# A transformer-like block on one core: the order of a turn's stages written out as two strings

## The reference, cut to what matters

```
x = x + attn_a(layernorm(x))   # 16 heads of 8 channels, softmax over all 1024 keys, output projection
x = x + ffn(layernorm(x))      # signs +-1 as weights: 128 -> 512 -> 512 -> 128, relu, scales s0, s1, s2
x = x + attn_b(layernorm(x))   # 8 heads of 16: for each token distances to the last 64 tokens under a learnt metric,
                               # the 32 nearest of them, weights exp(-distance), a weighted mean of values,
                               # a gate, times q, and a decoder matrix
x = x + ffn(layernorm(x))
```

## Time and profile before

| | |
|---|---|
| time, median of 3 runs | 2957.09 us (2952.42 to 2960.92) |
| profiled execution, span | 2956.4 us, 60895 instructions |
| PE busy | 2416.3 us (82%) |
| ACT busy | 2258.2 us (76%) |
| DVE busy | 2096.8 us (71%) |
| POOL busy | 732.5 us (25%) |
| phase one of TURN1 | 273.5 to 438.4 us |
| phases one of the six turns after it, sum | 1056.8 us |
| phases two of TURN1 to the last of `TURNS` (six), sum | 1025.5 us |
| phase two of TURN7 | 157.8 us |
| before TURN1, and the tail after TURN7 | 273.5 us and 277.9 us |

### The profile page before, as it was taken

The page is one execution under the profiler, slowest core; times in us unless marked ns, Lnnn a source line. Parts: engine busy times, 40 slices in busy tenths (PEclk is TensorE's granted clock), DMA queues, the critical chain, the costliest instruction groups (busy, mean ns, idle before and its releaser), DMA issues.

```text
span 2956.4 us, 60895 instructions
## 1 busy us (share of the span) xinstructions
PE 2416.3 (82%) x21171; PEld 1045.7 (35%) x21171; DVE 2096.8 (71%) x10258; ACT 2258.2 (76%) x3159; POOL 732.5 (25%) x933
## 2 busy tenths in 40 slices
PE   4788778888788887888888887888878888888666
PEld 1112233244332443334422443324433344324444
DVE  5801768957787668966799577876679666992585
ACT  4798668977699677987789776996769877895543
POOL 3020115211251114401162112511134111321442
PEclk6599789999899999999999998999989999999887
DMA  3011001100011001210011000110012000000000
GB/s 88 30 49 40 2 19 48 50 18 6 23 56 43 18 10 27 65 31 9 19 44 54 18 6 23 54 42 17 6 26 74 31 9 13 11 20 1 16 20 12
DMA packets 98519, 84.79 MB, mean 29 GB/s; under 512 B 19955, under 2 KB 79541, under 8 KB 98213
## 3 DMA queue, kind: packets, MB, share of 16 engines
q1 hardware_dynamic: 97968, 80.41, 9.3%
q10 hardware_dynamic: 244, 0.49, 0.1%
HBM read 55.32 MB, written 25.44 MB: 27 GB/s over the span
## 4 chain that ended last, share of the span: by engine, by line
PE 34%; ACT 34%; DVE 18%; issue 6%; POOL 6%; SPq 2%; DMA 1%; ACTq 0%; DVEq 0%; POOLq 0%
PE banks L849 31%; ACT PT L1188 17%; DVE xn L1535 4%; ACT pq L1175 3%; DVE h L1538 3%; DVE pq L1322 2%; ACT hparts L1199 2%; POOL Aop L820 2%; ACT h L1200 2%; ACT xn L1133 2%; PE banks L856 2%; ACT h L1101 1%; ACT Bs L1101 1%; POOL qkf L761 1%; DVE stat L1296 1%
## 5 line engine op out<-in xcount | busy, mean ns | idle before, releaser
L1188 ACT ACTIVATE PT<-banks 128x1024 f32<-128x1024 f32 x1024 | 996.6, 1038 | 51.0 <-PE banks L849 47.4
L1322 DVE CUSTOM_DVE_ANT_0 pq<-pq,banks 128x512 f32<-128x512 f32 x1024 | 653.5, 684 | 182.5 <-ACT pq L1175 182.0
L1175 ACT ACTIVATE pq<-banks 128x1024 f32<-128x1024 f32 x512 | 522.9, 1022 | 226.2 <-PE banks L849 201.0
L849 PE MATMUL banks<-PT,Vg 128*9 128x512 f32 x4096 | 545.0, 604 | 2.2 <-ACT PT L1188 2.2
L849 PE MATMUL banks<-Q,K 51*128 51x512 bf16 x2048 | 391.7, 393 | 139.7 <-ACT PT L1188 113.4
L849 PE MATMUL banks<-K,Q 48*128 48x512 bf16 x2048 | 361.6, 431 | 84.8 <-ACT pq L1175 38.0
L801 POOL TENSOR_TENSOR hparts<-h,hparts 128x512 fp32r<-128x512 f32 x108 | 135.6, 1272 | 995.2 <-ACT h L1200 995.2
L1535 DVE MATCH_REPLACE8 xn<-h,xn 128x96 f32<-128x96 f32 x1536 | 354.3, 256 | 0.0
L849 PE MATMUL banks<-hparts,W 128*128 128x512 f32 x992 | 291.4, 421 | 35.0 <-ACT h L1200 24.4
L849 PEld LDWEIGHTS banks<-Q,K 51*128 51x128 bf16 x2048 | 96.4, 93 | 619.1 <-ACT PT L1188 526.8
L1538 DVE MAX8 h<-xn 128x8 f32<-128x96 f32 x1536 | 264.3, 251 | 0.0
(11 more groups left out here) (217 smaller groups left out, 3330.6 us busy)
## 6 DMA issues: line engine op xcount, KB each, us to landing
Vw<-scratch_v SPq DMA_DIRECT2D x256, 51.0 KB, 2.1
scratch_k<-pq SPq DMA_DIRECT2D x24, 384.0 KB, 3.1
K<-scratch_k SPq DMA_DIRECT2D x126, 72.0 KB
qkf<-in_hidden_states SPq DMA_DIRECT2D x16, 512.0 KB, 4.4
scratch_q<-pq SPq DMA_DIRECT2D x24, 256.0 KB, 2.3
Q<-scratch_q SPq DMA_DIRECT2D x126, 48.0 KB
K<-scratch_k SPq DMA_DIRECT2D x126, 48.0 KB
scratch_v<-Bs SPq DMA_DIRECT2D x8, 544.0 KB, 3.6
```

The lines of the kernel that those rows point to most:

```text
L849: return pe.matmul(o, l, r, start=start, stop=stop)
L1175: act.activation(cut(g), ring_pair if work is TURN0 and g % 2 else pair[0], ACT.Relu).then_inc(diff_out.sem, 1)
L1188: act.activation(PT[:, at:at + 2, :], pair[g % ESLOTS], ACT.Exp, scale=1.0 if i % 8 < 4 else -1.0).then_inc(probs.sem, 1)
L1322: dve.tensor_tensor_reduce(r, r, pair[1 + g % 2][:, par, :], 1.0, -3.0e38, ALU.subtract, ALU.max, mred[:, par, i, qt:qt + 1]).then_inc(max ...
```

## The change

`phases` still merges the two parts as before. For the turns with sides behind (`behind`: TURN1, the five of `TURNS` and TURN7) each merged part is then re-ordered by a string. A letter names a line of work: `m` max and mrow, `t` mturn, `v` the value projections, `x` exp, `s` pvs and pvo (the eviction of a quad's result), `r` residual, `l` the four loads of `h`, and `o`, `p`, `q`, `h` the other stages of those sides. Within a line of work the order stays as it was; only how the lines are interleaved comes from the string. A letter with no line in this turn is skipped. Ring numbers are counted anew from the new list. No instruction is added or dropped.

```
+from collections import deque
...
+ORDER_ONE = (
+    "mqooqqoooqmooqomoqqmvqqqqmvooqqqqqqmooomoomqqqqqpomoooomoqqmqqmoqqqqmoqmqpmqmqqmqmqqmqqmpqqmqqqmpqqqqmqqqmppqqmq"
+    "qpmpqqmqmqqmpmpptmppppppmpppmmpppmppmppmpppmpmppmppppmpppqmptppmppppmppppmppmppmppmppmpmppmpppmptmppmpmppmppmppm"
+    "pppmppmppmppmppmppmpppmppmpppmm")
+ORDER_TWO = (
+    "hpxxpxxsxxhhsxxsxppxhhpppsxxpspxxphsxsppppxhxxpspxppxpssphxpxsptxxspxxpspppxxsxppppxhppsxxppphpxsxsxpxspsxxsxppp"
+    "xxsppxppsxpxpspppxsxppppxxpsxxsxxsspxppsxpxppxppsxpsppppxxppxppsxxsxpxsxxspsxpxsxxppppxssxxppppspppxppppxxspxxsx"
+    "xpppsxxsxxpssxpppxsxppppspphhxxpppxpsxxspxlxpspxxsppxxsxxppspsxxplpsxppxsppxxsxxppxsspxpxlxprpspxsxxpxsppspxxlpp"
+    "xssxpxxsxxsxxsxppxspsspp")
...
+def letter(work):
+
+    side, stage = work[:2]
+    if side == "a":
+        return dict(max="m", mrow="m", mturn="t", v="v", exp="x", pvs="s", pvo="s", residual="r")[stage]
+    return "l" if stage == "load" else side
+
+
+def woven(letters, order):
+
+    lines = {}
+    for work in order:
+        lines.setdefault(letter(work), deque()).append(work)
+    out = [lines[at].popleft() for at in letters if at in lines]
+    assert not any(lines.values()) and len(out) == len(order)
+    return out
...
     order = merged(*one) + merged(*two)
+    if behind:
+        order = woven(ORDER_ONE, merged(*one)) + woven(ORDER_TWO, merged(*two))
```

## The result

The changed kernel takes 2784.9 us (median of 4 runs, 2781.4 to 2791.3) against 2955.9 for the kernel before in the same runs: ratio 0.9434, 95% interval 0.9414 to 0.9455. The forecast was 2916, its range ended at 2872.

| us | before | after | change |
|---|---|---|---|
| six phases one with side `q` | 1056.8 | 974.7 | -82.1 |
| phase one of TURN1 | 164.9 | 152.3 | -12.6 |
| six full phases two | 1025.5 | 952.8 | -72.7 |
| phase two of TURN7 | 157.8 | 155.0 | -2.8 |
| ahead of TURN1, and the tail | 551.4 | 549.6 | -1.8 |

The account below looks back on a forecast made before the run. It took ACT to bound phase two and PE phase one. From 2957 us, phase two would give 48 and phase one cost 7, making 2916; the forecast's own range was 2895 to 2938, the full range 2872 to 2955.

Parts of the forecast that it names:

- 10.87 us of stalls: Phase two, first third: four ACT stalls, before `mT`, `xTa` and two exps, would all go, out of 16.5 us idle.
- The floor of 159 to 161: Full phase two: shortest length expected, ACT's 155.4 us of work plus 3.5 to 5.6 us of remaining idle time.
- Fifteen places: from 1 us (nearly all covered) to 7 us (none covered); I take 3.: Phase two: moved `pvs` stages would make ACT wait for PE, costing 3 us a phase, from 1 to 7.
- The lower bound of 30 us for phase two: Least total gain claimed for all phases two, whose forecast gain was 48 us with bounds 30 to 66.
- Cover: 4 us.: Phase boundary: the residual, biased by 164.3 us, would be ready 4 us before the next `wo` wants it at 168.
- Rival 4: Phase boundary: SP later than reckoned makes the residual late; 8 us late gives 2940 us; chance 0.03.
- which frees DVE of 2.15: Phase two, unit 4: moving POOL's bias add to the very end would spare DVE's stretched L1553 2.15 us.
- Taking the larger of the two engines and 1.79 in each interval gives 182.6 before and 183.9 after: Phase one, gaps between neighbouring `max` stages: a cost rule giving 1.3 us more a phase; 7 us booked in all.
- rival 3: Phase one: clumped side stages make PE wait at the ring, 9 us more in each of seven phases; 2972; chance 0.09.
- about 1 us each: Phase one: gain for each hand-over between side stages that stood back to back and now comes apart.
- The rival that phase one gains as well: Phase one: regrouped stages let PE work ahead of ACT, 5 us in each of seven phases; 2875; chance 0.17.
- The clock, counted as nothing in phase one: PE clock: about 1.3 us saved twice at phase two's `dist` was left uncounted; phase one's costing had no clock term.

Follow-up runs that it names:

- two_h: Kernel before with only side `h`, up to its third split, moved in phase two to the string's places; 2925.7 us, ratio 0.9920.
- two_pt: Kernel before with only side `p` and the last `mturn` moved in phase two to the string's places; 2918.3 us, ratio 0.9900.
- two_pth: Kernel before with side `p`, the last `mturn` and `h` up to its third split moved in phase two; 2877.1 us, ratio 0.9767.
- two_t: Kernel before with only the last `mturn` of phase two moved, from 3 to 22 exps ahead of it; 2949.6 us, ratio 0.9996.
- after_pvs: Changed kernel with `pvs` and `pvo` of phase two back at the old counts of exps; 2793.1 us, ratio 0.9476 to the kernel before.
- after_res: Changed kernel with the residual load moved up, ahead of the loads of quads; 2766.2 us, ratio 0.9382 to the kernel before.
- one_hand: Kernel before with seven `max` stages of phase one shifted to stand between seven back-to-back pairs of side stages; 2950.0 us, ratio 0.9997.
- one_only: Kernel before with the string for phase one alone, phase two keeping its merged order; 2849.2 us, ratio 0.9660.
- one_sides: Kernel before with phase one's side stages in the string's order, `max`, `mrow` and `mturn` keeping old counts of side stages ahead; 3016.2 us, ratio 1.0229.
- one_maxes: Kernel before with `max`, `mrow` and `mturn` of phase one at the string's counts of side stages ahead, side order old; 2894.8 us, ratio 0.9814.
- one_queue: Phase-one string alone, but three `max` stages moved from ahead of `lnn` to behind it; 2865.3 us, ratio 0.9725 to the kernel before.
- one_close: Phase-one string alone, but six `max` stages taken from between six pairs of side stages; 2872.1 us, ratio 0.9748 to the kernel before.
- one_hand2: Kernel before with ten phase-one `max` stages shifted: ahead of `lnn` and `lnT` at three layernorms, three more in quad 0; 2937.7 us, ratio 0.9959.
- one_sides2: Kernel before with phase one's side stages and `mturn` in the string's order, `max` and `mrow` keeping old counts; 2963.9 us, ratio 1.0058.

## Why the prediction was wrong

**Phase two, mechanism right.** 10.87 us of stalls were to leave; ACT's idle time fell by 10.4 a phase (15.5 to 5.1). The 33rd exp begins 45 to 46 us into a phase where it began 52 to 56 in: 6 to 11 of the 9 to 14 us that a phase is shorter lie ahead of it, and 2 to 3 more behind it. POOL's three hand-overs were the cause, as two_h, two_pt and two_pth show together; `mturn`, at which the largest stall stood, was not (two_t). The floor of 159 to 161 is where the phase ended: 158.8.

**The term that failed in phase two: "Fifteen places: from 1 us (nearly all covered) to 7 us (none covered); I take 3."** The sign was wrong. after_pvs shows +1.3 us a phase when the old places are put back. 163 less 3 less 1.3 is 158.7, the measured length, so this term is the whole miss in phase two (27 us in seven phases). I priced each place as if PE reached it at the same moment as ACT. Why none costs was not tried; one reading is that PE, freed of its stalls, is ahead of ACT there. The lower bound of 30 us for phase two was also added up wrongly: with 7 us paid back in each of seven phases its own terms leave 20 (and 62 with 1 us).

**The residual: "Cover: 4 us."** SP's queue was reckoned well: over the six phases the issue comes 152.9 to 156.3 us in (157 forecast), lands 5.8 to 7.4 us later (4.9 forecast), and the add ends at 161.6 to 165.6 (164.3 forecast). It was set against a phase two of 163 us, and the phase came out at 158.8: the 4 us that phase two gained beyond the forecast were the cover. Rival 4 gave a late residual a chance of 0.03, by a late SP; the shorter phase did it. The forecast also took the add's new place as free ("which frees DVE of 2.15"), and in four of six turns it cost about as much there. after_res prices both at 19 us.

**Phase one: the step "Taking the larger of the two engines and 1.79 in each interval gives 182.6 before and 183.9 after" failed.** It is responsible for 102 of the 131 us between 2916 and 2785 (+7 forecast, -94.7 measured). Its sum for before was already 6 us above the measured length of the list that it was to describe. (The 22 us of PE's waits in rival 3 and in the text on one_hand are low too: they sum to 26.0 in the phase at 956.9.) The same rule can be worked out for two more of the lists (estimates, with one cost for each kind of stage):

| list | rule, us a phase | measured |
|---|---|---|
| before | 182.6 | 176.1 |
| one_only | 183.9 | 158.8 |
| one_sides | 183.7 | 186.9 |
| one_maxes | 188.4 | 168.9 |

The first three lie within 1.3 us of each other where the measured ones span 28, and the one put last is the second fastest. The tight places it counted are no worse in the new order. PE's waits in a phase of before, and then of one_only (us in total, times, longest):

```profile
PE banks L849 <- ACT h L1200: 4.6, 5, 1.6
PE banks L849 <- ACT pq L1175: 4.4, 8, 1.0
PE banks L856 <- ACT xn L1133: 4.0, 3, 2.2
```

```profile
PE banks L897 <- ACT pq L1223: 4.2, 7, 1.0
PE banks L897 <- ACT h L1248: 2.5, 2, 1.6
...
PE banks L904 <- ACT xn L1181: 1.2, 1, 1.2
```

What the rule left out is the order inside an engine's queue: ACT's evictions, relus and `xn` are one list, and a `max` waits for its own bank's relu wherever DVE or PE has made ACT wait ahead of it. That is shown for the places that one_queue and one_close move, worth 27 and 31 us of the 104. Back-to-back pairs it knew only as "about 1 us each"; the costliest, `lnn` and `lnT` of (1,1), takes 2.16 us of PE before and none in one_only, where the `max` ahead of it waits 0.63 for a relu and 0.72 for DVE's maxima. The rival that phase one gains as well had 0.17 and a size of 5 us a phase; it was 13.5.

**The clock, counted as nothing in phase one.** From before to one_only PE's phase one loses 11.0 us of other time and 6.3 us of busy time with the same products. Windows of before, and then of one_only, the three lowest of the one and the lowest of the other (columns as in the earlier trace rows):

```profile
1302.10:1310.10 8.00, 6.04 (x34) 4.60 (x36) 3.75 (x17) 4.88 (x12) 0.00 (x0) 0.81 0.17 49
...
1438.10:1446.10 8.00, 8.00 (x26) 3.74 (x25) 2.36 (x9) 5.17 (x10) 0.84 (x1) 0.66 0.00 1
...
1462.10:1470.10 8.00, 7.23 (x46) 5.25 (x47) 6.43 (x13) 4.69 (x8) 0.34 (x1) 0.79 0.01 3
```

```profile
1375.50:1383.50 8.00, 6.49 (x25) 3.24 (x24) 6.03 (x24) 6.28 (x10) 0.00 (x0) 0.59 0.01 3
```

The 0.66 comes with the wait of 2.16 us at `lnT` (1,1), and PE shows a full 8.00 us of busy time in that window. So a stall on PE is paid for twice here: as idle time, and as slower products behind it.

**What stays open.** one_queue and one_close account for 27 and 31 of the 104 us in the six ones, partly at the same stages, and one_hand2 wins 23.5 from before's side. For the rest this is shown: it needs both the side order and the places of the maxes. The traces also say at which waits of PE it lies. Mean of the six phases one, us a phase, waits over 0.15 us by what ended them (`h` are ACT's evictions of the ffn's hidden layers, `on` is DVE's result that `back` turns):

| PE waits for | before | one_only | one_maxes | one_sides2 |
|---|---|---|---|---|
| ACT `h` | 7.7 | 3.4 | 6.9 | 6.1 |
| ACT `pq` (relu) | 4.6 | 4.2 | 7.1 | 7.5 |
| ACT `xn` | 3.8 | 1.2 | 1.0 | 3.9 |
| DVE `on` | 2.6 | 0.7 | 2.0 | 4.1 |
| all | 26.3 | 14.4 | 23.0 | 27.9 |

The largest part, 4.3 of 11.9 us, are waits for `h`, which no run isolates; the runs on ACT's queue dealt with `pq` and `xn` alone. Which pairs carry the `h` and `on` waits was not tried.

## What to carry to other kernels

When stages are queued on in-order engines, judge an order by each engine's own queue: for every stage ask which result its neighbour ahead on that engine still waits for, and move the short, needed work (here a relu that frees the next stage's banks) ahead of it. A sum of work per interval did not even rank four orders. A transfer's cover is to be worked out against the length that the change is to bring, and one with nothing to wait for is issued early. An add on POOL is also placed by what DVE runs beside it: late, it met a chain of tiny DVE instructions with PE waiting behind them; early, it met none that it stretched. The one move was 19 us here.

## What the runs showed of the hardware

**POOL's add and DVE.** In the kernel after, a POOL add of 128x1024 elements (2.35 to 2.37 us) lies near the phase boundary, beside DVE's chain `L1340` to `L1344` on 128x4 elements. The instruction of that chain which meets the add is stretched. L1340 at one boundary, where the add comes later, and at two where it does not, and L1341 at a fourth; all of the kernel after:

```profile
1228.78 0.15 DVE L1340 TENSOR_TENSOR ls<-ls 128x4 f32<-128x4 f32 x1
...
1868.64 0.94 DVE L1340 TENSOR_TENSOR ls<-ls 128x4 f32<-128x4 f32 x1
...
2188.99 2.18 DVE L1340 TENSOR_TENSOR ls<-ls 128x4 f32<-128x4 f32 x1
...
908.09 2.21 DVE L1341 TENSOR_TENSOR ls<-ls 128x4 f32<-128x4 f32 x1
```

Each ends within 0.03 us of its add (1869.56, 2191.15, 910.29), and so does L1342 at 585.98 above, which reads one tensor. With 2.44 against 0.29 in the earlier trace rows this is the same thing at another instruction. DVE instructions that read PSUM and at most one tensor of SBUF (L1442 `on<-banks,rden`, 0.29 us) are not stretched beside the add, nor are MAX8 and MATCH_REPLACE8 in after_res. The Trainium skill (GPSIMD Engine Reference, section 1, Specifications) has DVE and GpSimd contend for SBUF where DVE's instruction reads two inputs from it or runs in a 2-port perf mode. The trace agrees for the two inputs of L1340, L1341 and L1553; in which mode L1342 ran no trace shows. The add's new place did not free DVE of this, it gave the stretch to another instruction.

**The clock.** PE's other time and busy time in a phase one are 27.0 and 149.1 us before, 23.9 and 145.0 in one_maxes, 23.9 and 148.3 in one_hand2, 20.3 and 143.5 in one_close, 16.0 and 142.8 in one_only, 35.6 and 151.3 in one_sides. Busy time grows with other time, though not by its sum alone: the same 23.9 us go with 3.3 us more or less of busy time. Kernels that share before's list of phase one differ as well, from 147.7 to 149.8 us of busy time with 26.2 to 27.8 of other time, so that only about a third of the 3.3 is beyond that scatter; where the idle time lies may account for it, which was not tried.
